# Two position-dependent blurs: products and exponentials one row ahead of the sums, a 1x1 layer on row tiles, staging copies on one engine

## The reference

```python
h = relu(einsum('bchw,co->bohw', x, w1) + b1)              # 1x1 layer, 16 -> 32
ks = relu(einsum('bohw,o->bhw', h, w2[:, 0]) + b2[0]) * 20.0 + 1.0
sigma = ks / 3.0
wgt = exp(-gauss_kernel / (2.0 * sigma ** 2))              # 9x9 per pixel
wgt = wgt / wgt.sum over the 81 taps
low = sum over the 81 taps of wgt[tap] * shifted x         # same weights for all 16 channels
y = x + low
out = (y - mean(y over h, w)) / sqrt(var(y over h, w) + 1e-5)
```

## Time and profile before

| what | value |
|---|---|
| median of 3 runs | 536.21 us (534.25 to 538.63) |
| the profiled execution, its own time | 538.64 us |
| its span in the trace | 536.4 us |
| mean granted TensorE clock | 0.926 of full speed |
| busy: PE, DVE, ACT, POOL | 412.3 (77%), 340.5 (63%), 268.7 (50%), 181.5 (34%) us |

### The profile page before, as it was taken

The page is one execution under the profiler, slowest core; times in us unless marked ns, Lnnn a source line. Parts: engine busy times, 40 slices in busy tenths (PEclk is TensorE's granted clock), DMA queues, the critical chain, the costliest instruction groups (busy, mean ns, idle before and its releaser), DMA issues. The chain is left out here.

```text
span 536.4 us, 15849 instructions
## 1 busy us (share of the span) xinstructions
PE 412.3 (77%) x7024; PEld 292.8 (55%) x7024; DVE 340.5 (63%) x525; ACT 268.7 (50%) x298; POOL 181.5 (34%) x118
## 2 busy tenths in 40 slices
PE   4487988878999198668887886499965888887871
PEld 1177923217989122436665675377743466666760
DVE  2794586745888965336676786648433367777683
ACT  1665585653333000346787877411016386788581
POOL 3220022320000002137776794000030777777700
PEclk9879999997999789878999999879978799999897
DMA  8930000000000000022222220000000232332003
GB/s 188 187 138 1 1 1 1 0 1 1 2 2 3 1 0 0 2 79 83 83 82 82 84 81 4 3 1 0 0 1 25 96 122 83 82 83 82 4 4 156
DMA packets 17055, 24.83 MB, mean 46 GB/s; under 512 B 6735, under 2 KB 8544, under 8 KB 16864
## 3 DMA queue, kind: packets, MB, share of 16 engines
q1 hardware_dynamic: 15968, 23.52, 14.8%
q10 hardware_dynamic: 1024, 0.36, 0.4%
HBM read 21.53 MB, written 2.34 MB: 45 GB/s over the span
## 5 line engine op out<-in xcount | busy, mean ns | idle before, releaser
L1240 POOL TENSOR_TENSOR g_wgt<-g_exponents,g_s_wide 128x1024 f32<-128x1024 f32 x56 | 131.9, 2380 | 67.8 <-PE ps L977 34.0
L1083 ACT ACTIVATE g_wgt<-g_wgt 128x2048 f32<-128x2048 f32 x64 | 121.1, 1908 | 24.1 <-DVE g_wgt L1145 24.1
L977 PE MATMUL ps<-g_wgt,g_xt 128*32 128x64 f32 x4096 | 74.9, 224 | 25.3 <-issue 17.5
L977 PEld LDWEIGHTS ps<-g_wgt,g_xt 128*32 128x32 f32 x4096 | 63.9, 112 | 44.1 <-issue 31.5
L1145 DVE TENSOR_TENSOR g_wgt<-g_exponents,ps 128x1024 f32<-128x1024 f32 x72 | 84.9, 1202 | 2.6 <-PE ps L963 2.6
L1056 ACT ACTIVATE g_hid<-ps,vec 128x512 f32<-128x512 f32 x32 | 20.3, 684 | 85.2 <-PE ps L925 85.2
L1153 DVE COPY g_num<-ps 128x512 f32<-128x512 f32 x32 | 22.0, 688 | 56.0 <-PE ps L977 55.9
L963 PE MATMUL ps<-ident,g_scl 128*128 128x128 f32 x288 | 46.7, 302 | 4.0 <-DVE g_wgt L1145 2.7
L963 PEld LDWEIGHTS ps<-ident,g_scl 128*128 128x128 f32 x288 | 35.1, 151 | 9.0 <-DVE g_wgt L1145 4.0
L469 PE MATMUL ps<-conv_img,projblk 128*32 128x512 f32 x256 | 35.8, 681 | 0.0
L1439 PE MATMUL ps<-high,wb 128*128 128x512 f32 x72 | 30.5, 424 | 5.3 <-DVE rest L1468 5.3
(11 more groups left out here) (169 smaller groups left out, 731.1 us busy)
## 6 DMA issues: line engine op xcount, KB each, us to landing
g_s_wide<-g_s_rows SPq DMA_DIRECT2D x56, 256.0 KB, 3.7
x<-in_x SPq DMA_DIRECT2D x8, 256.0 KB, 6.9
x<-in_x SPq DMA_DIRECT2D x1, 2048.0 KB, 8.7
out<-g_result SPq DMA_DIRECT2D x4, 512.0 KB, 3.9
windows<-band SPq DMA_DIRECT2D x4, 256.0 KB, 5.3
g_s_rows<-g_srow SPq DMA_DIRECT2D x56, 4.0 KB
c_weight<-in_c_weight SPq DMA_DIRECT2D x1, 576.0 KB, 4.2
g_w<-in_g_w SPq DMA_DIRECT2D x2, 128.0 KB, 2.7
```

The costliest lines, as they stand in the source:

```text
L977: mm = pe.matmul(ps[32 * j:32 * j + 32, O_BANK, 64 * cb:64 * cb + 64], xt[(s + t) % 2][:, cb, b, :], weights_of(s, b)[:, t, cb, :], start= ...
L1083: act.activation(w, w, ACT.Exp).then_inc(weight, 1)
L1240: pool.tensor_tensor(weights_of(s, b), spread(gband[:].unsqueeze(2), shape), spread(s_wide[s][j][:].unsqueeze(1), shape), ALU.mult).then_i ...
```

## The change

- `pe_hidden`: matmul i reads only the 64 partitions of its own four images (`planes`), so the two matmuls sit on two row tiles of 64x128. For r >= 1 it waits for `small` 3r; the wait on the x copy starts at r = 2.
- `pe_xt` waits for the relu of the next row instead of the scale copy two rows on; `pe_ks_turn` waits for the x copy.
- The odd half of the staging is GpSimd's in all rows; `act_stage` and its semaphore go.
- The three orders are rewritten. In row r TensorE sums row r alone (both image halves, each half's two parts back to back), while VectorE, ScalarE and GpSimd make the products and exponentials of row r+1. The enhance and stats of a row come one row later on VectorE.

```diff
     def pe_hidden(pe, r):
-        if r == 1 or r == 2:
-            pe.wait_ge(xt_out, r)
-        elif r > 2:
+        if r >= 1:
+            pe.wait_ge(small, 3 * r)
+        if r >= 2:
             pe.wait_ge(xt_out, r - 1)
-            pe.wait_ge(small, 3 * r)
-        rows = slice(BLK * r + R, BLK * r + R + BLK)
         for i, bank in enumerate((MLP_BANK, XT_BANK)):
-            mm = pe.matmul(ps[:, bank, :], w1[:, i, :], pad[:, rows, R:R + W], start=True, stop=True)
+            planes = slice(64 * i, 64 * i + 64)
+            mm = pe.matmul(ps[:, bank, :], w1[planes, i, :], pad[planes, BLK * r + R:BLK * r + R + BLK, R:R + W],
+                           start=True, stop=True)
@@
     def pe_ks_turn(pe, r, s):
         pe.wait_ge(small, 3 * r + 2)
+        if r >= 1:
+            pe.wait_ge(xt_out, r)
@@
     def pe_xt(pe, g, s):
         pe.wait_ge(staged, g + 1)
-        if g >= 2:
-            pe.wait_ge(staged_a, g - 1)
-        pe.wait_ge(small, 3 * g + 3 if g < 2 else min(3 * g + 6, 3 * RB))
+        pe.wait_ge(small, min(3 * g + 4, 3 * RB))
@@
+    def pe_begin(pe):
+        pe_hidden(pe, 0)
+        pe_ks(pe, 0)
+        pe_ks_turn(pe, 0, 0)
+        for v in range(4):
+            pe_spread(pe, 0, 0, v)
+        pe_hidden(pe, 1)
+        pe_ks(pe, 1)
+        pe_xt(pe, 0, 0)
+        pe_spread(pe, 0, 0, 4)
+        pe_ks_turn(pe, 1, 1)
+        pe_spread(pe, 0, 0, 5)
+        pe_spread(pe, 0, 0, 6)
+        pe_hidden(pe, 2)
+        pe_ks(pe, 2)
+        pe_spread(pe, 0, 0, 7)
+        pe_xt(pe, 1, 1)
+        for v in range(3):
+            pe_spread(pe, 1, 1, v)
@@
     def pe_row(pe, r, s):
+        pe_blur(pe, r, s, 0, 0)
+        pe_blur(pe, r, s, 0, 1)
         if r + 2 < RB:
             pe_ks_turn(pe, r + 2, s)
         if r + 1 < RB:
             pe_spread(pe, r + 1, 1 - s, 3)
         if r + 3 < RB:
+            pe_hidden(pe, r + 3)
+        pe_turn(pe, r, 0)
+        if r + 2 < RB:
+            pe_spread(pe, r + 2, s, 0)
+        pe_blur(pe, r, s, 1, 0)
+        pe_blur(pe, r, s, 1, 1)
+        if r + 3 < RB:
             pe_ks(pe, r + 3)
+        if r + 2 < RB:
+            pe_spread(pe, r + 2, s, 1)
+        pe_turn(pe, r, 1)
+        if r + 2 <= RB:
+            pe_xt(pe, r + 2, s)
+        if r + 2 < RB:
+            pe_spread(pe, r + 2, s, 2)
+        pe_low(pe, r)
@@
-    def act_stage(act, g, s):
-        act.wait_ge(xt_mm, g - 1)
-        act.copy(*half_tile(g, s, 1)).then_inc(staged_a, 1)
@@
+    def act_begin(act):
+        act_hidden(act, 0)
+        act_square(act, 0)
+        act_hidden(act, 1)
+        act_square(act, 1)
+        act_xt(act, 0, 0)
         act_weight(act, 0, 0, 0)
+        act_hidden(act, 2)
         act_weight(act, 0, 0, 1)
+        act_square(act, 2)
         act_xt(act, 1, 1)
         act_weight(act, 0, 0, 2)
         act_weight(act, 0, 0, 3)
@@
     def act_row(act, r, s):
+        if r + 1 < RB:
+            act_weight(act, r + 1, 1 - s, 0)
         if r + 3 < RB:
             act_hidden(act, r + 3)
+        if r + 1 < RB:
+            act_weight(act, r + 1, 1 - s, 1)
+            act_weight(act, r + 1, 1 - s, 2)
+        if r + 3 < RB:
+            act_square(act, r + 3)
+        if r + 2 <= RB:
+            act_xt(act, r + 2, s)
+        if r + 1 < RB:
+            act_weight(act, r + 1, 1 - s, 3)
@@
+    def dve_begin(dve):
         dve_logit(dve, 0, 0, 0)
+        dve_relu(dve, 1)
         dve_logit(dve, 0, 0, 1)
+        dve_inverse(dve, 1, 1)
         dve_logit(dve, 0, 0, 2)
+        dve_scale(dve, 1, 1)
         dve_logit(dve, 0, 0, 3)
+        dve_relu(dve, 2)
         dve_logit(dve, 0, 0, 4)
         dve_inverse(dve, 2, 0)
+        for v in range(5, B):
+            dve_logit(dve, 0, 0, v)
@@
     def dve_row(dve, r, s):
+        if r + 1 < RB:
+            dve_logit(dve, r + 1, 1 - s, 0)
+        if r >= 1:
+            dve_enhance(dve, r - 1)
+        if r + 1 < RB:
+            dve_logit(dve, r + 1, 1 - s, 1)
         if r + 2 < RB:
             dve_scale(dve, r + 2, s)
+        dve_num(dve, r, 0)
+        if r + 1 < RB:
+            dve_logit(dve, r + 1, 1 - s, 2)
+        dve_mix(dve, r, 0)
+        if r >= 1:
+            dve_stats(dve, r - 1)
+        if r + 1 < RB:
+            dve_logit(dve, r + 1, 1 - s, 3)
+        dve_num(dve, r, 1)
+        if r + 3 < RB:
+            dve_relu(dve, r + 3)
+        dve_mix(dve, r, 1)
+        if r + 3 < RB:
+            dve_inverse(dve, r + 3, 1 - s)
@@
     def pool_stage(pool, g, s):
         if g >= 2:
             pool.wait_ge(xt_mm, g - 1)
-        else:
-            pool.tensor_copy(*half_tile(g, s, 1))
+        pool.tensor_copy(*half_tile(g, s, 1))
         pool.tensor_copy(*half_tile(g, s, 0)).then_inc(staged, 1)
```

More of the change, by code:

```diff
@@ L870, in blur @@
     staged = sem("staged")
-    staged_a = sem("staged_a")
     xt_mm = sem("xt_mm")
@@ L1000, in pe_low @@
         tr.then_inc(low_mm, 1)
-    def pe_first_row(pe):
+    def pe_begin(pe):
[7 more added lines that the diff above has]
+        pe_xt(pe, 0, 0)
         pe_spread(pe, 0, 0, 4)
+        pe_ks_turn(pe, 1, 1)
         pe_spread(pe, 0, 0, 5)
-        pe_ks_turn(pe, 1, 1)
         pe_spread(pe, 0, 0, 6)
+        pe_hidden(pe, 2)
+        pe_ks(pe, 2)
         pe_spread(pe, 0, 0, 7)
         pe_xt(pe, 1, 1)
-        pe_hidden(pe, 2)
-        pe_ks(pe, 2)
-        pe_spread(pe, 1, 1, 0)
-        pe_spread(pe, 1, 1, 1)
-        pe_ks_turn(pe, 2, 0)
-        pe_blur(pe, 0, 0, 0, 0)
-        pe_spread(pe, 1, 1, 2)
-        pe_hidden(pe, 3)
-        pe_blur(pe, 0, 0, 0, 1)
-        pe_spread(pe, 1, 1, 3)
-        pe_ks(pe, 3)
+        for v in range(3):
+            pe_spread(pe, 1, 1, v)
     def pe_row(pe, r, s):
-        pe_blur(pe, r - 1, 1 - s, 1, 0)
-        pe_turn(pe, r - 1, 0)
+        pe_blur(pe, r, s, 0, 0)
+        pe_blur(pe, r, s, 0, 1)
         if r + 2 < RB:
             pe_ks_turn(pe, r + 2, s)
-        pe_blur(pe, r - 1, 1 - s, 1, 1)
-        if r + 1 < RB:
-            pe_spread(pe, r + 1, 1 - s, 0)
-            pe_spread(pe, r + 1, 1 - s, 1)
-        if r < RB:
-            pe_xt(pe, r + 1, 1 - s)
-        pe_turn(pe, r - 1, 1)
-        if r < RB:
-            pe_blur(pe, r, s, 0, 0)
-        if r + 1 < RB:
-            pe_spread(pe, r + 1, 1 - s, 2)
-        if r + 3 < RB:
-            pe_hidden(pe, r + 3)
-        if r < RB:
-            pe_blur(pe, r, s, 0, 1)
-        pe_low(pe, r - 1)
         if r + 1 < RB:
@@ L1083, in act_weight @@
         act.activation(w, w, ACT.Exp).then_inc(weight, 1)
-    def act_stage(act, g, s):
-        act.wait_ge(xt_mm, g - 1)
-        act.copy(*half_tile(g, s, 1)).then_inc(staged_a, 1)
-    def act_first_row(act):
+    def act_begin(act):
[4 more added lines that the diff above has]
+        act_xt(act, 0, 0)
         act_weight(act, 0, 0, 0)
-        act_square(act, 1)
+        act_hidden(act, 2)
         act_weight(act, 0, 0, 1)
+        act_square(act, 2)
         act_xt(act, 1, 1)
-        act_stage(act, 2, 0)
-        act_hidden(act, 2)
-        act_square(act, 2)
         act_weight(act, 0, 0, 2)
-        act_hidden(act, 3)
         act_weight(act, 0, 0, 3)
     def act_row(act, r, s):
-        if r + 2 < RB:
-            act_square(act, r + 2)
-        act_weight(act, r, s, 1)
-        act_weight(act, r, s, 0)
-        act_xt(act, r + 1, 1 - s)
-        if r + 2 <= RB:
-            act_stage(act, r + 2, s)
-        act_weight(act, r, s, 3)
+        if r + 1 < RB:
+            act_weight(act, r + 1, 1 - s, 0)
         if r + 3 < RB:
             act_hidden(act, r + 3)
-        act_weight(act, r, s, 2)
+        if r + 1 < RB:
[7 more added lines that the diff above has]
+            act_weight(act, r + 1, 1 - s, 3)
     def dve_relu(dve, r):
@@ L1293, in _ @@
                 pe.wait_ge(a, 16)
-            pe_hidden(pe, 0)
-            pe_ks(pe, 0)
-            pe_ks_turn(pe, 0, 0)
-            for v in range(4):
-                pe_spread(pe, 0, 0, v)
-            pe_xt(pe, 0, 0)
-            pe_hidden(pe, 1)
-            pe_ks(pe, 1)
+            pe_begin(pe)
             pe.wait_ge(const_ready, 4)
-            pe_first_row(pe)
-            for r in range(1, RB + 1):
+            for r in range(RB):
                 pe_row(pe, r, r % 2)
@@ L1309, in _ @@
             act.wait_ge(band_ready, 1)
-            act_hidden(act, 0)
-            act_square(act, 0)
-            act_xt(act, 0, 0)
-            act_hidden(act, 1)
-            act_first_row(act)
-            for r in range(1, RB):
+            act_begin(act)
+            for r in range(RB):
                 act_row(act, r, r % 2)
@@ L1341, in _ @@
             dve.wait_ge(band_ready, 2)
-            dve_first_row(dve)
-            for r in range(1, RB + 1):
+            dve_begin(dve)
+            for r in range(RB):
                 dve_row(dve, r, r % 2)
+            dve_enhance(dve, RB - 1)
+            dve_stats(dve, RB - 1)
             dve.wait_ge(stat, RB)
```

28 lines of the change are left out of this document (removed).

## The result

The changed kernel takes **517.18 us**, the median of 4 runs (515.45 to 519.72); the kernel before took 536.64 beside it (4 runs, 534.25 to 538.63). The ratio is 0.964 [0.959, 0.970]. So it is faster, but by 19.5 us where 48 were forecast, and outside the range given (480 to 504). The profiled execution took 519.72 us, its span is 517.5 us.

A forecast was written before the change was run, and what follows sets the result against it. Bound: a closed chain of 13.24 us a row, sums standing with that row's own products and exponentials. Gains 26.2 + 27.9 = 54.1, less 5.5 for stalls, take 538.64 to 490.0; median 2.4 lower, 488 us, range 480 to 504.

The forecast's parts named there:

- the forecast 73.5: Rows of each blur, first pair to row 7's pair: 54.0 + 19.5 = 73.5 us, against 91.3 and 92.5 before.
- term for stalls: TensorE stalls without any waited semaphore: 5.5 us added, about eight per run at 1.4, half in spare time.
- the sum without stalls: Whole kernel's profiled execution with both blurs' gains of together 54.1 us and no stalls added: 484.5 us.
- "The row after" (1) to (3): Blur row: VectorE's products, ScalarE's exponentials and square, then VectorE's reciprocal close a loop of 10.8 us.
- that rival (493): Hidden layer's row tiles don't overlap or cost: rows 11.05 to 11.25 us, total 493 us; chance 0.13.
- GpSimd does not bind: Blur rows: rival that GpSimd becomes the bound, 11.6 us a row over seven rows, total 503 us; chance 0.13.
- (5): GpSimd in a blur row: needs 10.55 us, inside the row's 10.8.
- TensorE's row: TensorE's work in a blur row: two pairs, transposes, ks turn and hidden layer, 9.2 to 10.1 us.
- 512 by that mechanism: Blur rows: a misjudged wait ties sums to the same row's exponentials, row stays 12.5 or so, some 512; chance 0.06.
- "The start": Start of the first blur, first hidden layer to first pair: 24.4 us, first pair at 236.0, 7.3 us sooner.
- "The sum": Both blurs: gains 26.2 and 27.9, together 54.1 us, less 5.5 for stalls; median forecast 488 us.
- The last rival: TensorE short of instructions at the pair heading each row: 5 us stalls, 15.1 a row, 549 us; chance 0.03.

The follow-up runs named there:

- half-records run: Changed kernel with one 128-column matmul in place of two of 64 in the sums, the second block using the first's window: 489.17 us, ratio 0.913.
- after: The changed kernel with the whole change, against the kernel before: 517.18 us, ratio 0.964.
- the repeated run: The changed kernel measured once more, unedited, beside other versions on the same chip: 518.09 us, ratio 0.970 to the kernel before.
- the run with spaced loads: Changed kernel with SyncE issuing the `s_wide` loads one by one over the row from row 3 on: 513.11 us, ratio 0.957 to the kernel before.

## Why the prediction was wrong

**What held.** The mechanism of the change was read rightly, term by term. In the half-records run, where TensorE streams the same columns with its instructions in time, the rows of both blurs take 73.6 us from the first pair to row 7's, against the forecast 73.5, and the ends 9.7 against 9.6:

```profile
238.71:312.35 73.64, 65.51 (x1244) 53.77 (x1244) 64.08 (x100) 65.57 (x52) 72.94 (x40) 1.00 0.29 89
392.75:466.37 73.62, 65.32 (x1243) 53.75 (x1243) 64.07 (x100) 65.55 (x52) 68.02 (x39) 1.00 0.28 89
```

From first hidden layer to last statistics the two blurs take 217.6 us there, and 217.0 in the forecast before its term for stalls. That its 489 and the forecast 488 are so near is luck all the same: the forecast holds 5.5 us of stalls and this run none. Of the 2.8 us by which its profiled execution is over the sum without stalls (487.27 against 484.5), 1.9 stand ahead of the first blur. The loop of "The row after" (1) to (3), with the reciprocal waiting 0.5 to 0.6 us for the square, gives 10.77 for 10.8. The row tiles overlap: 1.13 us, so that rival (493) is out. GpSimd does not bind in after, where long rows give it time, though at 10.77 busy of 10.77 in the half-records run its 10.55 of (5) was 2% low and it stands level with the loop. TensorE's row was put too low, 9.2 to 10.1 for a measured 10.50, which left 0.3 us of spare time in place of the forecast 0.7. The order does run ahead, so 512 by that mechanism is out too, though 517 is near it. The staging's move costs nothing, as said.

**"The start"** was 1 to 2 us short: 26.65 us for 24.4. Some of it goes with TensorE's clock. In the profiled execution the second hidden layer lasts 1.86 us, and the mean clock of the whole start is 0.81; in the repeated run it lasts 1.18, the start 25.3, and the mean clock is 0.87.

```profile
210.87:237.50 26.63, 17.63 (x122) 11.71 (x122) 15.53 (x19) 12.23 (x14) 10.05 (x12) 0.81 0.12 42
```

**The step that failed is in "The sum": the 5.5 us for stalls,** "about eight per run at 1.4, half of it in spare time". Each of its three parts was off. The stalls were 15 or 16 in number, not eight; they lasted 1.8 us in the mean (26.8 / 15), not 1.4; and almost none was in spare time. The mis-sized term measured 27 to 29 us. After minus the half-records run is 518.09 - 489.17 = 28.9 us, against 28.5 us of stalls in that after's trace: they go into the time about one to one. What the change did is to make them more and longer (11.9 to 26.8 us). It joined the halves of the sums, so that 256 records stand in 1.9 us where the old order had 128 and then other work; and it cut the rows to where TensorE had 0.3 us left (10.50 busy of 10.77), so hardly a stall has cover.

The working had both facts before it: the pair as x128 in 1.99 us, and a stall of 3.08 in a run of the same instruction. The last rival named the mechanism, "TensorE runs short of instructions", with a chance of 0.03. But it was priced as a stall in every row, and only as the way to a slower kernel. Between "5.5 us in all" and "4.3 in each row" nothing was priced, and that is where the result lies: 30.2 us over the 14 rows of the table, 2.2 in the mean, in rows that alternate between two stalls and none at first, while both last rows of the first blur and six of the second's seven hold one or two. Its argument against, that the clean row of 13.21 has no unseen wait, took as a proof of supply a row whose block boundaries lay in a harmless place. That "today the stalls have cover" was wrong too: without them the kernel before is 13.8 us faster. And the place given, the head of the pair, was wrong: they come where a block ends, mostly near a pair's end.

**A second effect of a stall** is on the clock. Behind the 3.00 us wait at 306.04 the next window of the changed kernel has a mean granted clock of 0.80, between TensorE's 1.2 and 2.4 GHz, and eight transposes of the windows take nearly twice their 1.04 (the row at 270.11 of the same trace):

```profile
306.04:314.42 8.38, 6.42 (x127) 5.76 (x128) 4.32 (x6) 4.14 (x3) 8.38 (x4) 0.80 0.01 2
```

```profile
270.11 1.04 PE L950 MATMUL ps<-ident,g_tile 128*128 128x128 f32 x8
...
308.08 1.91 PE L950 MATMUL ps<-ident,g_tile 128*128 128x128 f32 x8
```

So that stall is followed by a loss of its own. The same place looks alike in two more traces: a mean clock of 0.73 over the 3.65 us behind a stall of 3.26 in the repeat of after, 0.80 behind one of 2.44 in the run with spaced loads. And in the half-records run, whose rows have no stall, the clock is 1.00 over all rows of both blurs (the two windows above), where after has 0.96 and 0.92. That the stall is what lowers the clock is argued from this, not shown by a run that lengthens one. The rows of the second blur, at 0.92, lost 15.8 us, those of the first, at 0.96, 14.4.

**What stays open.** Why the packets start late. TensorE goes on 1.2 to 1.6 us after the landing each time, so the length of a stall hangs mostly on when its packet starts, and that is 0 to 6.1 us after TensorE has crossed the boundary before. A burst of loads holds it back at 303.85; but the one of 312.10, the latest of all, has no other transfer within 7 us ahead of it. Whether the blocks could be asked for earlier wasn't tried.

## What to carry to other kernels

Count instructions, not only their time: where an engine issues hundreds of records at under 10 ns each (256 in 1.9 us here), and a denser order takes away its waits, the stream of instructions itself becomes a resource, and "issue" gaps at multiples of one distance in record numbers are its signature, and a packet of the instruction queue that lands shortly before the engine goes on shows it outright. A short trial with half the records and the same columns tells in one run what supply costs. An idle gap in the trace of before that no semaphore explains should be priced on its own: how often it comes, what decides its place, and whether the new order still has cover for it.

## What was not expected of the hardware

- TensorE was fed in blocks of 256 instructions (one packet of 16 KB in the page's queue of instructions) and went on from a stall 1.2 to 1.6 us after one had landed; blocks used up in 1.9 to 2.0 us ended in stalls of 0.7 to 2.4 us, and half the records for the same columns left none in either blur.
- With loads of 256 KB each, four in a row, ahead of it such a stall lasted 3.00 us, with small loads 1.12; its packet of instructions started when the loads' burst ended.
- Two matmuls of 512 columns on row tiles 64x128, four records, took 1.13 us against 1.88 on full tiles.
- 128 columns in one record took as long as 64 in two: 1.95 and 1.99 us a pair. The finer cut bought nothing but records.
